# A graph network in one kernel: two PSUM banks for the product of layer 0, one for the copy of the rounded rows, and turn, product and readings two chunks later

## What is computed

```python
agg = segment_sum(x[src], dst, num_segments=N)
h = (1.0 + eps) * x + agg
h = relu(batch_norm(h @ W1 + b1, g1, be1))      # 512 -> 1024
h = relu(batch_norm(h @ W2 + b2, g2, be2))      # 1024 -> 512
x = layernorm(x + (x + h))
```

```python
agg = segment_sum(x[src], dst, num_segments=n)
h = where(indeg > 0, agg, x)
h = relu(h @ W.T + b)
x = layernorm(x + batch_norm(h, gamma, beta))
```

## Time and profile before

| | us |
|---|---|
| median of 3 runs | 2989.48 |
| lowest, highest | 2987.55, 3002.36 |
| the profiled execution | 3012.35 |
| its span, first to last instruction | 3010.6 |
| PE busy in it | 2427.2 (81%) |
| POOL, DVE, ACT busy | 1548.7, 1370.1, 955.1 |
| mean granted TensorE clock | 0.894 of 2.4 GHz |

### The profile page before, as it was taken

One profiled execution on the slowest core, in us unless ns is written; L12 is line 12 of the kernel. 1 busy time (PEld: TensorE's weight loads), 2 busy tenths in 40 slices (PEclk: granted clock), 3 DMA queues, 4 the chain that ended last, 5 costly groups with the idle time before them and its releaser, 6 DMA issues. The chain is left out here.

```text
span 3010.6 us, 42654 instructions
## 1 busy us (share of the span) xinstructions
PE 2427.2 (81%) x9711; PEld 1615.2 (54%) x9712; DVE 1370.1 (46%) x2159; ACT 955.1 (32%) x1674; POOL 1548.7 (51%) x1729
## 2 busy tenths in 40 slices
PE   3888778788887887799997497888779788877875
PEld 2555555556565655578886354444444444444445
DVE  4444444444443444453336554444344444444448
ACT  2444444444443443455555311010111011011026
POOL 6555656656555565500001465666566666666633
PEclk9989989999988898899998598989889898988986
DMA  7666656666666666632225765666666666666668
GB/s 242 183 194 185 206 170 203 191 204 188 202 184 195 181 205 184 184 94 95 95 95 151 248 189 171 184 183 177 177 180 181 190 183 183 188 180 180 175 175 270
DMA packets 180572, 545.12 MB, mean 181 GB/s; under 512 B 48787, under 2 KB 51178, under 8 KB 175794
## 3 DMA queue, kind: packets, MB, share of 16 engines
q0 software_dynamic: 125120, 410.09, 47.1%
q1 hardware_dynamic: 33880, 78.23, 8.8%
q10 hardware_dynamic: 21544, 56.48, 5.7%
HBM read 493.06 MB, written 51.62 MB: 181 GB/s over the span
## 5 line engine op out<-in xcount | busy, mean ns | idle before, releaser
L821 PE MATMUL psum<-ring,select 128*125 x2600 | 1270.1, 616 | 36.6 <-issue 36.4
L571 POOL DMA_INDIRECT ring<-x_in,staged x782 | 742.5, 950 | 522.9 <-issue 206.2
L571 POOL DMA_INDIRECT ring<-x_d,staged x782 | 751.3, 961 | 459.5 <-issue 219.7
L821 PEld LDWEIGHTS psum<-ring,select 128*125 128x125 f32 x2600 | 492.7, 196 | 440.7 <-issue 397.1
L854 PE MATMUL psum<-sumsT_hi,w_hi 128*128 128x250 f32 x1248 | 429.2, 344 | 244.8 <-ACTq L949 146.8
L670 DVE TENSOR_TENSOR rows_lo<-ring,psum 128x512 fp32r<-128x512 f32 x404 | 274.6, 686 | 425.4 <-ACT psum L931 352.5
L854 PEld LDWEIGHTS psum<-sumsT_hi,w_hi 128*128 128x128 f32 x1248 | 273.3, 219 | 318.7 <-ACTq L949 179.2
L929 ACT ACTIVATE rows_hi<-ring 128x512 fp32r x506 | 315.1, 628 | 315.0 <-issue 220.7
L854 PE MATMUL psum<-sumsT_lo,w_hi 128*128 128x250 f32 x1248 | 384.3, 308 | 7.0 <-issue 7.0
L854 PE MATMUL psum<-sumsT_hi,w_lo 128*128 128x250 f32 x1248 | 383.1, 307 | 7.6 <-issue 7.4
L806 PE MATMUL psum<-rows_hi,select_r 128*125 128x512 f32 x500 | 359.3, 719 | 13.1 <-issue 9.9
(11 more groups left out here) (184 smaller groups left out, 2470.9 us busy)
## 6 DMA issues: line engine op xcount, KB each, us to landing
hidden_d<-of_layer ACTq DMA_DIRECT2D x25, 1000.0 KB
act_f<-hidden_d SPq DMA_DIRECT2D x24, 1000.0 KB
ring<-x_in,staged POOLq DMA_INDIRECT x782
ring<-x_d,staged POOLq DMA_INDIRECT x782
own<-x_in ACTq DMA_DIRECT2D x50, 224.0 KB
own<-x_d ACTq DMA_DIRECT2D x50, 224.0 KB
rows_r<-x_in SPq DMA_DIRECT2D x6, 1120.0 KB
x_d<-rows_r SPq DMA_DIRECT2D x6, 1120.0 KB
```

The costliest lines, as they stand in the source:

```text
L571: nc.gpsimd.indirect_dma_start(slot(s), None, table, bass.IndirectOffsetOnAxis(ap=staged[:, s:s + 1], axis=0)).then_inc(gathered[s], 16)
L821: whole = nc.tensor.matmul(agg(h), select[h][:, WHOLE_AT.index(p), :], of_chunk(pe, first, place), start=False, stop=n + 1 == WINDOW, skip ...
```

## The change

In layer 0 the product's parts use banks 4 and 7 in turn (`prod_ps`), `PRODUCT_BANKS` is 2, and part b+1 waits for the reading of part b-1. The second copy of the rounded rows has bank 5 alone (`high_ps`), and `AHEAD` is 1: ACT may write row k when DVE has subtracted row k-1. Turn and all four parts stand two chunks later in PE's order. On ACT the reading of part 0 follows four rows of tile 1 where it followed three, with the load of `own` for tile 1 ahead of it; the later readings move by one to two rows as well. On DVE the six first rows of tile 1 now stand ahead of the sums of tile 0, and the last two ahead of the statistics. The last product after the loop uses banks 4 and 7 where it used 4 and 0.

```diff
-    TURN_AT = 5
-    PRODUCT_AT = ({14: 0}, {2: 1, 8: 2, 14: 3}) if layer == 0 else ({12: 0}, {2: 1})
+    TURN_AT = 7 if layer == 0 else 5
+    PRODUCT_AT = ({16: 0}, {4: 1, 10: 2, 16: 3}) if layer == 0 else ({12: 0}, {2: 1})
...
-        high_ps = [m.bank(5), m.bank(7)]
-        AHEAD = 2 if layer == 0 else 0
-        assert SPLIT % 2 == 0
-        PRODUCT_BANKS = 1 if layer == 0 else 2
-
-        def prod_ps(b, last):
-
-            return m.bank(4 if b % 2 == 0 or layer == 0 and not last else 0 if layer == 0 else 5)
+        high_ps = m.bank(5)
+        AHEAD = 1 if layer == 0 else 0
+        PRODUCT_BANKS = 2
+
+        def prod_ps(b):
+
+            return m.bank(4 if b % 2 == 0 else 7 if layer == 0 else 5)
...
-                            low_rows(v, 1, second, 0, 3)
+                            low_rows(v, 1, second, 0, 6)
                             read_sums(v, tiles(i, 0), 0)
-                            low_rows(v, 1, second, 3, 5)
...
                         if layer == 0:
-                            statistics(v, pair, 0, 2)
-                            low_rows(v, 1, second, 5, 7)
-                            statistics(v, pair, 2, 4)
-                            low_rows(v, 1, second, 7, SPLIT)
+                            low_rows(v, 1, second, 6, SPLIT)
+                            statistics(v, pair, 0, 4)
                             low_rows(v + 1, 0, following, 0, 2)
...
-                    pe.wait_ge(product_out, HALVES * job + b + (1 if layer == 1 or b == 0 or not final else 0))
+                    pe.wait_ge(product_out, HALVES * job + b + 1)
...
                             high_rows(begin, v, 0, first, 6, SPLIT)
-                            high_rows(begin1, v, 1, second, 0, 3)
+                            high_rows(begin1, v, 1, second, 0, 4)
+                            load_own(v, tiles(i, 1), 1)
                             read_product(v, pair, 0)
-                            high_rows(begin1, v, 1, second, 3, 5)
-                            load_own(v, tiles(i, 1), 1)
+                            high_rows(begin1, v, 1, second, 4, 6)
                             read_product(v, pair, 1)
-                            high_rows(begin1, v, 1, second, 5, 7)
+                            high_rows(begin1, v, 1, second, 6, SPLIT)
...
                         if layer == 0:
+                            high_rows(following_begin, v + 1, 0, following, 0, 2)
                             read_product(v, pair, 2)
-                            high_rows(begin1, v, 1, second, 7, SPLIT)
-                            high_rows(following_begin, v + 1, 0, following, 0, EARLY)
+                            high_rows(following_begin, v + 1, 0, following, 2, EARLY)
                             read_product(v, pair, 3)
```

More of the change, by code:

```diff
@@ L668, in low_rows @@
                         dve.wait_ge(split_hi, SPLIT * (2 * v + h) + k + 1)
-                        high = high_ps[k % 2] if layer == 0 else rows_hi[:, k, :].bitcast(F32)
+                        high = high_ps if layer == 0 else rows_hi[:, k, :].bitcast(F32)
                         nc.vector.tensor_tensor(rows_lo[:, k, :], of_chunk(dve, first, SPLIT_AT[k]), high, ALU.subtract
@@ L841, in turn, with product @@
                     last.then_inc(turned, 1)
-                def product(job, b, final=False):
+                def product(job, b):
                     if b == 0:
@@ L846, in product @@
                         pe.wait_ge(weights_lo, W_PARTS)
-                    pe.wait_ge(product_out, HALVES * job + b + (1 if layer == 1 or b == 0 or not final else 0))
+                    pe.wait_ge(product_out, HALVES * job + b + 1)
                     for o in (2 * b, 2 * b + 1):
-                        out = prod_ps(b, final)[:, (o % 2) * z.W:(o % 2 + 1) * z.W]
+                        out = prod_ps(b)[:, (o % 2) * z.W:(o % 2 + 1) * z.W]
                         parts = [(w, s, k) for k in range(z.KD)
@@ L885, in _ @@
                 for _ in range(14):
-                    nc.tensor.matmul(prod_ps(0, True)[:, 0:z.D], w_hi[:, 0, 0:P], w_hi[:, 0, 0:z.D], start=True, stop=True)
+                    nc.tensor.matmul(prod_ps(0)[:, 0:z.D], w_hi[:, 0, 0:P], w_hi[:, 0, 0:z.D], start=True, stop=True)
                 for b in range(HALVES):
-                    product(uses, b, final=True)
+                    product(uses, b)
                 if layer == 0:
@@ L930, in high_rows @@
                         if layer == 0:
-                            high = nc.scalar.activation(high_ps[k % 2].bitcast(F32R), of_chunk(act, first, SPLIT_AT[k]),
+                            high = nc.scalar.activation(high_ps.bitcast(F32R), of_chunk(act, first, SPLIT_AT[k]),
                                                         ACT.Copy)
@@ L940, in read_product @@
                     for o in (2 * b, 2 * b + 1):
-                        from_ = prod_ps(b, last)[:, (o % 2) * z.W:(o % 2 + 1) * z.W]
+                        from_ = prod_ps(b)[:, (o % 2) * z.W:(o % 2 + 1) * z.W]
                         if layer == 0:
```

## The result

The changed kernel takes 2968.68 us (median of 6 runs, 2962.90 to 2973.22) beside 2991.85 us for the kernel before on the same chip (6 runs, 2987.55 to 3002.36). The ratio is 0.9927, with a 95% interval of 0.9906 to 0.9948: faster by 0.7%, where 3058 us and a slower kernel had been forecast.

The account below looks back on a forecast made before the run. The prediction took ACT and DVE alternating at the rounded rows as the bound: 43.8 + 4.2 + 4.8 = 52.8 us per pair against 50.04, +69 us on 2989.5, giving 3058 us, range 2955 to 3140.

Parts of the forecast that it names:

- The chain of 43.8 us: Layer 0's loop: ACT and DVE alternate at rounded rows, 36.8 us plus other work, 43.8 us per pair.
- The product's wait goes: Line 854, PE waiting for ACT before a product part: two banks give back at most 5.9 us per pair.
- what goes wrong on the chain: Holds and late words on ACT and DVE in layer 0's loop: 4.2 plus 4.8 us per pair added.
- The late word for the sums: DVE's sums waiting for a late word: between 0 and 4.8 us per pair, taken whole.
- the shift: Turn and product two chunks later with their readings: distances stand, so it costs nothing by itself.
- the holds: "Issue" waits at ACT's rows, DVE's rows and DVE's low part: between 0 and 4.2 us per pair, taken at 4.2.
- The 0.74 us of "issue" before the high part: On ACT before the turn's high part at 611.87: 0.74 us of "issue", shown as a hold.
- The late words on the readings: Line 943, ACT's reading of a part: between 0 and 19.2 us per pair, taken at 0.
- point of decision: ACT and DVE together must come below about 49 us per pair, needing more than 3.8 of 9.0 to fall away.
- the rival "faster": Layer 0's chain keeps slack and product waits go: 2842 us at best, 2916 at half; chance 0.13.
- what would show it: Signs in layer 0's loop: stores 52 to 54 us apart if right, 45 to 49 with long product waits if wrong.
- the chain had slack: Layer 0's loop, sign of being wrong: stores 45 to 49 us apart and ACT still waiting long for products.

Follow-up runs that it names:

- a2: The changed kernel run again, unaltered, on a second prompt chip: 2645.64 us, 1.0583 of the kernel before.
- i3: The changed kernel with turn, product and readings back in the order of before, on a late chip: 3015.89 us, 1.0026 of the kernel before.
- g2: The kernel before with only the rounded rows' second copy put in one bank, on a late chip: 3065.54 us, 1.0143 of the kernel before.
- i1: The changed kernel run again, unaltered, on a late chip: 2988.36 us, 0.9935 of the kernel before.
- c1: The kernel before with layer 0's column numbers for DVE's selections read from SBUF, on a late chip: 2962.21 us, 0.9923 of the kernel before.
- c4: The kernel before with column numbers read from SBUF and the new order added, on a late chip: 2983.77 us, 0.9981 of the kernel before.
- g1: The changed kernel with layer 0's product cut to weights high times sums high, on a late chip: 2997.51 us, 0.9919 of the kernel before.
- e1: The kernel before with only the rounded rows' second copy put in one bank, on a prompt chip: 2645.85 us, 1.0597 of the kernel before.
- c2: The kernel before with column numbers in SBUF, the new order and product banks 4 and 6, keeping two copy banks: 2950.40 us, 0.9862 of the kernel before.
- e3: The kernel before with only turn, product and readings two chunks later, on a prompt chip: 2497.47 us, 0.9997 of the kernel before.
- f3: The kernel before with only the new order, run again on a second prompt chip: 2496.75 us, 0.9994 of the kernel before.

## Why the prediction was wrong

**The chain of 43.8 us: right.** A row costs 2.30 us in the result, and where nothing goes wrong the changed kernel's loop took 43.79 us, against 43.8 summed from single rows. That the two agree so closely is luck in part. In one pair of `a2`, 601.39 to 645.28 us, the distances between ACT's rows exceed 2.30 us by:

| us over 2.30 | predicted | in the pair |
|---|---|---|
| selection of tile 1 | 1.37 | 1.21 |
| sums of tile 0, register load, next selection | 2.79 | 2.23 |
| high part of the turn | 0.64 | 1.01 |
| part 0 with the loads of `own` | 0.61 | 0.49 |
| parts 1 and 2 | 0.11 | 0.02 |
| part 3, store, turn of the loop | 1.51 | 1.44 |
| at rows that the list does not name | 0 | 0.69 |
| sum | 7.03 | 7.09 |

**The product's wait goes: right** (146.8 us to no row). That ACT then comes to its readings later than the word does was nearly right: 404.3 us became 52.4, not 0.

**The step that failed is "what goes wrong on the chain"**, the 9.0 us per pair put on top whole, where 4.96 were measured (48.75 on the late chip less 43.79 on the prompt one). Its terms are:
- The late word for the sums, taken at 4.8, was worth 0.1. The row of DVE's sums over the 24 periods of the changed kernel:

```profile
L684 DVE SCALAR_TENSOR_TENSOR sums<-own,self_weight,psum 125x512 f32<-125x512 f32 x48 | 35.7, 744 | 16.7 <-issue 13.7 <-remote 2.5 <-PE psum L817 0.5
```

and with the order undone (`i3`):

```profile
L685 DVE SCALAR_TENSOR_TENSOR sums<-own,self_weight,psum 125x512 f32<-125x512 f32 x48 | 35.8, 747 | 41.5 <-remote 25.0 <-issue 14.7 <-PE psum L821 1.9
```

Over the 24 periods the kernel before has 115.3 us of this wait (121.0 in the earlier trace rows), the alternation alone (`g2`) 37.9, with the bank (`i3`) 25.0, and with the order as well 2.5, or 3.6 on the chip of `i3` (`i1`); before, `g2`, `i3` and the result come from different late chips. The order does it by itself too, 101.0 to 2.3 from `c1` to `c4`. I read it so: DVE, slowed by the alternation, comes to its sums later, and `low_rows(v, 1, second, 0, 6)` puts three more rows of 2.30 us ahead of `read_sums`. The prediction had used this argument for ACT's readings (the engine comes later than the word, so the word costs nothing) and not for DVE's sums, where it held as well. The diff showed the moved rows; the prediction looked only at the distances between turn, parts and readings when it priced the shift at nothing.
- Of the holds, taken at 4.2, no more than the 2.8 of rows and high part above reached the period. What of them is hold and what is late rows of DVE the traces do not part. The 0.74 us of "issue" before the high part, which the prediction showed as a hold, is no sign of one: on the prompt chip, where ACT's rows have 9.4 us of "issue" in all, the high part has 29.8 / 24 = 1.24 us per pair.
- The late words on the readings, taken at 0, were 2.1.

The forecast's own point of decision was that more than 3.8 of the 9.0 fall away; 9.0 - 4.96 = 4.0 did. So it was the rival "faster" that came true, at its edge, and the 0.13 given to it was too little for a term whose bounds were 0 and 9.0: taking both open terms at their upper end was the choice that decided the sign.

**The second product bank** was given no gain of its own, because the chain was to be the bound. On prompt chips that was right (0.2 us per pair or less). On late chips it is worth 2.3 us per pair in the changed kernel, and without it that kernel would have been slower by 1.7%. That is an estimated 3042 us (2991.85 x 1.0167), near the forecast: its sum describes the kernel with the product in one bank better than the one it was made for.

**Of what would show it**: ACT's rows waiting for several hundred us (201.6, and more under "issue"), no product wait above 30 and late words below 150 all came true while the kernel was faster and not slower. Two signs told the cases apart. The stores: 48.75 lies in the 45 to 49 that the prediction had named for "the chain had slack", though ACT did not still wait long for products, as it had said beside it. And PE, which should have waited more in total, was idle less: 1170.0 - 970.8 = 199 us over the 24 periods, where it had been 1201.0 - 976.9 = 224.

## What to carry over

Where a kernel waits for words that arrive late, a second buffer can be worth more than where they are prompt (here 70 us against nothing), and an added chain can cost less (45 us against 148). Price a late word by whether its waiter will come before or after it, at each place by the same rule, and count how many rows the change puts ahead of each waiter. A loop that stands at 50 us on one chip and at 38 on another has two bounds, and a change can gain against one and lose against the other: here one chip's measurement alone would have given the opposite advice.

## What the runs showed of the hardware

**Two kinds of chip.** The same kernel before took 2498 us on two chips and 2989 to 3021 us on the others. Of the 322 us by which the profiled executions of the changed kernel differ (2967.4 and 2645.2), (48.75 - 43.79) x 25 = 124 lie in layer 0's loop, and the rest outside it. TensorE's mean granted clock differs too (0.952 on the prompt chip, 0.908 on the late one; in the loop 0.96 and 0.93), but on the late chip PE is not what the loop's period waits for: `g1` took two thirds of the product away and gained nothing. What the clock does to the stages outside the loop was not looked into.

**Counts of TensorE that arrive late.** I lay each record of a product's count between 54 and 1290 us beside the last modelled end of such a matmul ahead of it. The mean distance is 4.4 us in the kernel before (96 records), 3.7 in the changed one and 3.5 in `i1`; the median is 0.01 us in `a2` and `e1` on prompt chips. The chunks' counts laid so are 1.3 to 1.9 us late in the mean on late chips, in all kernels but `g1` (0.8 and 0.9), and 0.01 on prompt ones. These are lower figures: on late chips some counts have no record of their own (342 records for the 400 split chunks of the changed kernel, 403 in `a2`), and laid the other way, from each end to the next record, the means are up to 5.7 us for the product and 2.6 to 3.5 for the chunks. Why is open.

The prediction had weighed instruction fetch (the Trainium skill, "Runtime: NRT & Kernel Launch", Instruction fetch mechanics: a taken branch that leaves the fetched window stalls its engine). By that rule the holds belong to the code; but the same code runs almost without them on a prompt chip (9.4 us of "issue" before ACT's rows in `a2`, 259.1 in the result), and `g1`, with fewer instructions, keeps them. Its product's counts are 2.8 to 4.6 us late, by the two ways of laying. So that rule alone does not explain them. A fetch that takes longer on one kind of chip, and a test with less gather traffic, were not tried.

**A table of numbers moved from PSUM to SBUF** gained 0.8% on a late chip (`c1`), with no count of instructions changed and no row found that explains it. What the trace does show is a price: a gather on POOL that runs beside a selection by DVE takes 1.25 us in the mean when the selection reads both its operands from SBUF, and 0.947 when it reads one of them from PSUM.

**The best kernel here** is `c2` on a late chip, 2950 us. It was not run on a prompt one, where the kernels that keep two banks for the copy (`e3`, `f3`) stand at 2497.
